# Two keys prepared at the start of the recurrence and split by VectorE, and buffers kept from the recurrence into attention

## What is computed

```python
x = _layernorm(x + _L0_attn_ref(x, ...))              # a selective-scan recurrence (Mamba)
x = _layernorm(x + _L0_xattn_ref(x, ctx, ctx, ...))   # cross attention, 16 heads of 16
x = _layernorm(x + _L0_ffn_ref(x, ...))               # 15 experts, top 3, and a shared expert

# the recurrence: E = 512 channels, N = 16 states, 256 steps
h = exp(d_l[:, :, None] * A) * h + (d_l * x_l)[:, :, None] * B_l[:, None, :]
y_l = einsum('ben,bn->be', h, C_l)

# cross attention
q, k = apply_rope(q), apply_rope(k)                   # x * cos + rotate_half(x) * sin
Q, K, V = q @ Wq.T + bq, k @ Wk.T + bk, v @ Wv.T + bv
out = softmax(Q K^T / sqrt(16)) V;  return out @ Wo.T + bo
```

## Time and profile before

| | |
|---|---|
| median of three executions | 1957.96 us |
| the profiled execution: its time / its span | 1956.72 / 1954.8 us |
| TensorE, VectorE, ScalarE, GpSimd busy | 83%, 76%, 55%, 65% of the span |
| recurrence, from the first scan | 61 to about 943 us |
| attention block | 958 to about 1440 us with the first part of the shared expert |
| feed forward | to the end |
| mean granted TensorE clock | 0.93 of 2.4 GHz |
| DMA | 239 MB, 122 GB/s over the span |

### The profile page before, as it was taken

The page is one execution under the profiler, slowest core; times in us unless marked ns, Lnnn a source line. Parts: engine busy times, 40 slices in busy tenths (PEclk is TensorE's granted clock), DMA queues, the critical chain, the costliest instruction groups (busy, mean ns, idle before and its releaser), DMA issues. The chain is left out here.

```text
span 1954.8 us, 32722 instructions
## 1 busy us (share of the span) xinstructions
PE 1627.6 (83%) x9596; PEld 1045.3 (53%) x9597; DVE 1481.9 (76%) x2438; ACT 1083.9 (55%) x2436; POOL 1266.4 (65%) x942
## 2 busy tenths in 40 slices
PE   7777777788878777874389989998997999999997
PEld 5444444444544444442156666665675556555686
DVE  4999999999999999989668878886532444444478
ACT  4777777777777877775235544444321333333325
POOL 3888888899888889898446888883410333333300
PEclk9789999989899998896689999998998999999999
DMA  7455555444454554444446764442145222222262
GB/s 236 115 117 119 120 130 130 107 110 94 103 126 113 130 130 115 103 97 93 88 125 168 196 185 138 137 136 69 67 177 187 87 84 86 85 85 87 72 263 87
DMA packets 180374, 239.35 MB, mean 122 GB/s; under 512 B 24778, under 2 KB 116813, under 8 KB 178158
## 3 DMA queue, kind: packets, MB, share of 16 engines
q1 hardware_dynamic: 160110, 201.04, 39.5%
q0 software_dynamic: 9888, 27.80, 4.0%
q10 hardware_dynamic: 10240, 8.84, 1.8%
HBM read 173.19 MB, written 65.90 MB: 122 GB/s over the span
## 5 line engine op out<-in xcount | busy, mean ns | idle before, releaser
L348 POOL TENSOR_TENSOR inject<-dx_n,bc_n 128x2048 f32<-128x2048 f32 x127 | 576.0, 4548 | 94.0 <-issue 67.3
L533 ACT ACTIVATE ps_h<-delta_n,a_neg 128x256 f32<-128x256 f32 x1024 | 425.0, 463 | 114.4 <-DVE hc L703 78.6
L690 DVE TENSOR_TENSOR_SCAN ps_h<-ps_h,inject 128x1024 f32<-128x1024 f32 x160 | 365.7, 2286 | 21.0 <-ACT ps_h L533 21.0
L1510 ACT ACTIVATE expT<-ps_t 128x512 f32<-128x512 f32 x256 | 148.5, 596 | 190.2 <-PE ps_t L1995 185.9
L357 POOL TENSOR_TENSOR h_pool<-h_pool,bc_n 128x1024 f32<-128x1024 f32 x96 | 227.2, 2368 | 0.0
L1636 DVE TENSOR_REDUCE neg_max<-ps_s 128x2 f32<-128x512 f32 x256 | 172.4, 680 | 71.4 <-PE ps_s L1984 65.1
L690 DVE TENSOR_TENSOR_SCAN h_pool<-ps_h,inject 128x1024 f32<-128x1024 f32 x96 | 218.5, 2276 | 3.4 <-ACT ps_h L533 3.4
L2641 PE MATMUL ps_uh<-arena,s_xT 128*128 x440 | 210.3, 601 | 5.0 <-issue 4.9
L703 DVE TENSOR_TENSOR hc<-ps_h,bc_n 128x1024 f32<-128x1024 f32 x160 | 195.7, 1223 | 5.9
L2481 DVE TENSOR_TENSOR s_gate<-ps_uh,arena 128x512 f32<-128x512 f32 x110 | 76.1, 692 | 138.6 <-PE ps_uh L2641 138.6
L2370 ACT ACTIVATE s_act<-ps_aa 128x256 f32<-128x256 f32 x110 | 42.3, 384 | 189.8 <-PE ps_aa L2648 189.8
(11 more groups left out here) (332 smaller groups left out, 3387.9 us busy)
## 6 DMA issues: line engine op xcount, KB each, us to landing
delta_n<-dup_rows SPq DMA_DIRECT2D x124, 256.0 KB, 4.6
dx_n<-dup_rows SPq DMA_DIRECT2D x124, 256.0 KB, 7.4
bc_n<-bc_rows SPq DMA_DIRECT2D x64, 256.0 KB, 4.5
xg<-slot_rows SPq DMA_DIRECT2D x110, 136.0 KB, 2.1
Qs<-q_rows SPq DMA_DIRECT2D x192, 64.0 KB, 2.7
arena<-token_results SPq DMA_DIRECT2D x8, 1536.0 KB, 18.5
Ks<-k_rows SPq DMA_DIRECT2D x180, 64.0 KB, 2.7
dup_rows<-delta SPq DMA_DIRECT2D x32, 256.0 KB, 3.7
```

What stands on the lines that cost most here:

```text
L348: nc.gpsimd.tensor_tensor(inject[:, at:at + 2, :, :], dx_n[c // 2][:, None, :, c % 2, :].to_broadcast([P, 2, JB, L]), bc_n[b % 2][:, 0, nq ...
L533: last = nc.scalar.activation(ps_h[k % 2][:, j, :], delta_n[c // 2][:, j, c % 2, :], ACT.Exp, scale=a_neg[:, c, nq, j:j + 1])
L690: nc.vector.tensor_tensor_scan(out.rearrange("p j t -> p (j t)"), ps_h[k % 2][:, :, :].rearrange("p j t -> p (j t)"), inject[:, k % RING, ...
L1510: nc.scalar.activation(expT[:, h % (2 * HG), :, :], ps_t[h % 2][:, :, :], ACT.Exp).then_inc(h_exp, 1)
```

## The change

- `AHEAD` is 2: at the recurrence's beginning two keys are made instead of three. GpSimd only rotates them; VectorE splits both. VectorE's list is now make_dx(0,0), refine(REST), the two splits, make_dx(0,1), first scan. ScalarE computes the root for refine(REST) ahead of `take_k`. One context load fewer is issued.
- At the recurrence's end VectorE splits query 1 too, ahead of the last layer norm's steps; GpSimd ends with the rotations.
- A tensor `common` lives from the recurrence into attention (and its room is reused in feed forward). In the recurrence it holds u[0], skip[0], delta_n[0] and dx_n[0]; in attention cos, sin, Wq, Wk, Qs[0] and Ks[0]. So SP loads cos, sin, Wq and Wk once, during the last sequence, and issues the 12 stack DMAs of key 0 and the first 6 of query 0 (after saving it, and before saving query 1) before the recurrence's block ends. SP waits for each query's save.
- In attention the four `turn_loads` and ScalarE's stacks are gone; ACT's queue issues context 2, context 0, Wv, bv and context 3. GpSimd clears the V buffers, then rotates key 2, splits it (query 2 was its work before), and rotates key 3.
- Key 2 is made in round -1: `project_k(2)` at h 5, `project_q(2)` at h 7 (was 5), `turn_max(0, 0)` at 13 (was 11). Work of round -1's end moves into round 0: `project_v(0)` to h 1, `turn_max(0, 1)` to h 2, `turn_x(3)` to h 3, `project_k(3)` from h 3 to 6 and `project_q(3)` from 5 to 8. VectorE splits query 2 at h 1 of round 0, takes V at 3, rotates query 3 at 5, and splits the output bias at 9, 11, 13, 15 (was 2, 4, 6, 8). SP issues the loads of Wo and bo ahead of two context loads and saves key 2.
- Feed forward: the same instructions on buffers that lie elsewhere.

```diff
@@ recurrence: SP
+            sp.wait_ge(s_inject, inject_count((B - 1) * ITERS + ITERS // 2 - 1))
+            for c in range(DC):
+                stack(qk.Ks, c, qk.k_dram, K_ORDER)
+            sp.wait_ge(s_decay, (B - 1) * ITERS + ITERS // 2)
+            save_q(0)
+            stack(qk.Qs, 0, qk.q_dram, Q_ORDER)
+            save_q(1)
@@ recurrence: GpSimd, begin and end
-            g.wait_ge(qk.got, 16 * 8)
+            g.wait_ge(qk.got, 16 * K_LOADS)
             for n in range(AHEAD):
...
-            split_k(0)
             for p in range(LEAD):
                 make_injects(p)
             g.wait_ge(qk.k_split, AHEAD)
...
-            g.wait_ge(qk.q_made, MADE)
-            g.wait_ge(s_hc, hc_count(B * ITERS - 1))
-            split(q_rows[1], q_parts[1], qk.q_split)
@@ recurrence: ScalarE
             take_delta(0, 0)
+            root(REST, 2)
             take_k(0)
             take_k(1)
             softplus_exp(0, 1)
             softplus_log(0, 1)
             take_delta(0, 1)
-            take_k(2)
-            root(REST, 2)
@@ recurrence: VectorE
             make_dx(0, 0)
+            refine(REST, 2)
+            for n in range(AHEAD):
+                v.wait_ge(qk.kb_made, n + 1)
+                split(k_rows[n], k_parts[n], 18 + 4 * n, qk.k_split)
             make_dx(0, 1)
-            refine(REST, 2)
-            for n in range(1, AHEAD):
-                v.wait_ge(qk.kb_made, n + 1)
-                split(k_rows[n], k_parts[n], 18 + 4 * (n - 1), qk.k_split)
@@ recurrence: TensorE
             project_k(0)
             project_k(1)
             add_softplus(0, 1)
-            project_k(2)
             transposes(1)
@@ attention: SP, GpSimd, ACT
-            stack_q(0, 0)
             stack_q(0, 1)
-            load_ctx(AHEAD)
-            load_ctx(0)
...
-            g.wait_ge(turn_got, TURN)
-            k_rope(AHEAD)
+            for q in range(2):
+                link(nc.gpsimd.memset(V[q][:, :, :, :], 0.0))
+                nc.gpsimd.memset(V[q][:, :, :, DK:DK + 1], 1.0).then_inc(pads_set, 1)
+            k_rope(2)
             split_max(0, 0)
-            split_q(2)
+            split_k(2)
             split_max(0, 1)
+            k_rope(3)
...
-            act.wait_ge(k_saved, 16)
-            stack_k(0)
-            for dst, src in turn_loads:
-                act.dma_start(dst, src).then_inc(turn_got, 16)
-            stack_k(1)
+            act.dma_start(ctxT[2][:, :, :], ctx_v[2]).then_inc(ctx_in[2], 16)
+            act.dma_start(ctxT[0][:, :, :], ctx_v[0]).then_inc(ctx_in[0], 16)
+            for dst, src in late_loads:
+                act.dma_start(dst, src).then_inc(late_got, 16)
+            act.dma_start(ctxT[3][:, :, :], ctx_v[3]).then_inc(ctx_in[3], 16)
+            take_k(2)
             take_q(2)
             take_max(0, 0)
-            take_max(0, 1)
@@ attention: VectorE
-            v.wait_ge(turn_got, TURN)
             rope_q(2)
             add_rope(2)
...
+                    if b == 0 and h == 1:
+                        split_q(2)
+                    if b == 0 and h == 3:
+                        v.wait_ge(late_got, LATE)
+                        take_v(0)
@@ attention: TensorE
                     if b == -1 and h == 5:
-                        pe.wait_ge(turn_got, TURN)
+                        project_k(2)
+                    if b == -1 and h == 7:
                         project_q(2)
+                    if b == 0 and h == 1:
+                        pe.wait_ge(late_got, LATE)
+                        pe.wait_ge(kb_made, 3)
+                        project_v(0)
+                    if b == 0 and h == 3:
+                        pe.wait_ge(v_made, 1)
+                        turn_x(3)
+                    if b == 0 and h == 6:
+                        project_k(3)
+                    if b == 0 and h == 8:
+                        pe.wait_ge(n_made, 2)
+                        project_q(3)
```

More of the change, by code:

```diff
@@ L115, in mamba_phase @@
         zcor = skip_raw
-        u = [sb(f"u{j}", [P, EC, L]) for j in range(2)]
-        skip = [sb(f"skip{j}", [P, EC, L]) for j in range(2)]
+        u = [qk.common[0][:, 0, :, :], sb("u1", [P, EC, L])]
+        skip = [qk.common[0][:, 1, :, :], sb("skip1", [P, EC, L])]
         db = sb("db", [ZK, L])
@@ L123, in mamba_phase @@
         dx = sb("dx", [P, 2, L])
-        delta_n = [sb(f"delta_n{j}", [P, JB, 2, L]) for j in range(2)]
-        dx_n = [sb(f"dx_n{j}", [P, JB, 2, L]) for j in range(2)]
+        delta_n = [qk.common[1][:, :, :, :].rearrange("p a c t -> p (a c) t").rearrange("p (j c) t -> p j c t", c=2),
+                   sb("delta_n1", [P, JB, 2, L])]
+        dx_n = [qk.common[2][:, :, :, :].rearrange("p a c t -> p (a c) t").rearrange("p (j c) t -> p j c t", c=2),
+                sb("dx_n1", [P, JB, 2, L])]
         bc_n = [sb(f"bc_n{j}", [P, 2, NQ, L]) for j in range(2)]
@@ L182, in mamba_phase @@
         EXP_A = 3
+        K_LOADS = 7
         def roots_at(n):
@@ L310, in _, with stack, save_q @@
                                      ).then_inc(qk.k_saved, 16)
+            def stack(to, c, of, order):
+                of_v = of[0].rearrange("(h d) (c a t) -> d c h a t", d=DK, c=DC, a=PARTS)
+                for i, part in enumerate(order):
+                    sp.dma_start(to[i * DK:(i + 1) * DK, c * HC:(c + 1) * HC, :], of_v[:, c, :, part, :]
+                                 ).then_inc(qk.stacked[c], 16)
+            def save_q(n):
+                sp.wait_ge(qk.q_split, n + 1)
+                sp.dma_start(qk.q_dram[n], q_parts[n].rearrange("p c a t -> p (c a t)")).then_inc(qk.q_saved, 16)
+                sp.wait_ge(qk.q_saved, 16 * (n + 1))
             sp.wait_ge(out_done, B - 1)
@@ L807, in _ @@
             v.wait_ge(s_hc, hc_count(B * ITERS - 1))
-            split(q_rows[0], q_parts[0], 18 + 4 * (AHEAD - 1), qk.q_split)
+            for n in range(MADE):
+                if n:
+                    v.wait_ge(qk.q_made, n + 1)
+                split(q_rows[n], q_parts[n], 18 + 4 * (AHEAD + n), qk.q_split)
             for step in rows:
@@ L1173, in __init__ @@
         self.bq, self.bk = sb("bq", [P, DC]), sb("bk", [P, DC])
+        self.whole = sb("common", [P, 3, 2, EC, L])
+        self.common = [self.whole[:, j, :, :, :] for j in range(3)]
+        self.Qs, self.Ks = (self.whole[0:SR + PARTS, j, :, :, :].bitcast(BF16).rearrange("p a c t -> p (a c t)").rearrange(
+            "p (h t) -> p h t", h=NH) for j in (1, 2))
+        self.stacked = [sem(f"stacked{c}") for c in range(DC)]
         self.got, self.chain = sem("got"), sem("chain")
@@ L1197, in sem @@
             return ctx.enter_context(nc.semaphore(name))
-        wq, wk, wv, wo = (sb(n, [P, DC, D]) for n in ("wq", "wk", "wv", "wo"))
+        cos, sin, wq, wk = (front.common[0][:, j // 2, j % 2 * DC:(j % 2 + 1) * DC, :] for j in range(4))
+        wv, wo = sb("wv", [P, DC, D]), sb("wo", [P, DC, D])
         bq, bk = front.bq, front.bk
         bv = sb("bv", [P, D])
-        cos, sin = sb("cos", [P, DC, L]), sb("sin", [P, DC, L])
         ident_bf = sb("ident_bf", [P, P], BF16)
@@ L1621, in set_pads @@
             def set_pads():
-                for q in range(2):
-                    nc.vector.memset(V[q][:, :, :, :], 0.0).then_inc(pads_set, 1)
                 nc.vector.tensor_copy(ident_bf[:, :], ident[:, :]).then_inc(pads_set, 1)
@@ L2105, in _ @@
                         turn_max(b + 1, 0)
-                    if b == -1 and h == 15:
-                        pe.wait_ge(n_made, 1)
-                        turn_max(0, 1)
                     if real(b - 2) and h == 13:
```

147 lines of the change are left out of this document (66 added, 81 removed).

## The result

The changed kernel took 1939.39 us, median of ten executions (1936.31 to 1948.69), against 1956.94 us for the kernel before on the same chip (ten executions, 1952.03 to 1965.91). The ratio is 0.9918, with a 95% interval from 0.9897 to 0.9939: 16 us less, between 12 and 20. The forecast was 11.6 us less, and its range of 1938 to 1952.5 holds the measured time, 1.4 us from its lower end.

What follows compares the result with a forecast made beforehand. The prediction took VectorE to set the recurrence's steady pace and TensorE attention's, both untouched by the change. It summed 1956.72 - 5.7 + 0.5 - 6.4 = 1945.1 us, range 1938 to 1952.5.

Steps and rivals of the forecast that it cites:

- third pair: Recurrence's beginning: GpSimd's third pair of input terms starts at 55.4 instead of 61.17 us, its 5.75 us wait gone.
- Term 1: Recurrence's beginning: VectorE's 10.3 us lead is cut to about 6 by iteration 7; -5.7 us, from -5 to -10.3.
- the lead is kept whole: Rival: recurrence keeps VectorE's 10.3 us, or attention its whole 9 to 11 us; 1940.5 or 1938 us, chance 0.14.
- Recurrence's end: VectorE's split of query 1 and SP's serial list of saves and stacks cost +0.5 us, from 0 to +1.5.
- the first part: Attention's start up to the first exponential: the 12.25 us wait goes, first exponential 9.0 us earlier (-9.0).
- The second part: Attention's round 0, first exponential to take_max of the next sequence: moved-in work less the bo wait, +2.6 us.
- the bo wait: Attention's round 0: VectorE's 3.94 us wait for bo goes, since Wo and bo are issued earlier.
- attention gives nothing: Rival: in round 0 split_q(2) and GpSimd's rotation of key 3 delay each other, 3.9 us; 1951.5 us, chance 0.15.
- the 12.25 us wait: Attention's start: VectorE waits 12.25 us for Wk to land before rotating query 2; claimed to go.
- Nothing is gained anywhere: Rival: the beginning's lead is lost at a sequence boundary where GpSimd waits for dx; 1957 us, chance 0.09.
- Slower: Rival: moved buffers cost GpSimd time in the recurrence, instructions 13% longer, 4 us of loss; 1961 us, chance 0.06.

Runs made afterwards that it cites:

- e1: Changed kernel with project_db(1) put ahead of the sums in iteration 4 of the first sequence; ratio to the kernel before 0.9884 (0.9842 to 0.9926).
- e9: Changed kernel with project_db(1) ahead of the sums, bo's split in round -1 and turn_max(0, 0) at head 11; median 1931.59 us, ratio 0.9877 to the kernel before.
- e3: Changed kernel with cos, sin, Wq and Wk loaded again at attention's start; one execution, 1958.6 us (whole time not used); block to first exponential 28.4 us.
- e5: Changed kernel with bo and Wo loaded at attention's start and bo split at head 5 of round -1; ratio to the kernel before 0.9911 (0.9887 to 0.9934).
- e6: Changed kernel with only bo's split moved, to heads 0, 2, 4 and 5 of round 1; ratio to the kernel before 0.9933 (0.9915 to 0.9952).
- e4: Changed kernel with key 0's stacks issued at attention's start again; one execution, 1957.98 us (whole time not used); block to first exponential 31.2 us.
- e11: The changed kernel itself, unchanged, run again in a later group; median 1938.20 us, ratio to the kernel before 0.9908 (0.9890 to 0.9927).
- e10: Changed kernel with e9's three edits, sequence 3's rotation and projection one head earlier, and maxima (1, 1) split before key 4's rotation; 1931.79 us, ratio 0.9876 to kernel before.
- e2: Changed kernel with refine(REST) put back behind the splits and make_dx(0,1); one execution, 1953.16 us (whole time not used); lead at scan 16 5.2 us.

## Why the prediction was right, and where its working was off

**Recurrence's beginning: right in mechanism, and in size partly by luck.** Forecast: first scan 48.6, third pair 55.4, ScalarE's db near 74, a lead cut from 10.3 to about 6 by iteration 7. Measured: 49.45, 56.1 (51.60 plus one pair of 4.53), 74.61, and 10.3 cut to 7.0 at iteration 7 and 6.3 at 10. The first two are 0.7 to 0.9 late because dx landed at 46.97 instead of 46.29. Term 1 was -5.7 and is -6.3. Two errors cancel in it: the chain that was to carry 5.7 us carried 5.0, and 1.2 us that ScalarE had waited for VectorE behind `db` in the kernel before went too, which the working didn't count. The choice between the two numbers was the largest choice in the sum; e1 shows it was decided by the chain that was named, as that lead stays at 9.4 once `project_db` no longer stands behind GpSimd's product. The rival "the lead is kept whole" named this chain as what speaks against it, and that held.

From scan 50 on the lead wanders: 4.0 at scan 56, then 3.2, 5.6, 5.1, and 7.4 at the last scan. The windows of single sequences show why, in the kernel after and then before (us; busy time of PE, PEld, DVE, ACT and POOL; granted clock, DMA share, GB/s):

```profile
163.60:218.80 55.20, 44.16 (x276) 26.32 (x273) 52.39 (x48) 43.20 (x96) 48.41 (x14) 0.91 0.51 115
218.80:276.30 57.50, 45.46 (x276) 26.46 (x276) 52.55 (x48) 43.56 (x96) 50.90 (x15) 0.91 0.51 113
276.30:332.60 56.30, 46.79 (x279) 27.63 (x280) 52.50 (x48) 43.00 (x96) 50.28 (x16) 0.88 0.49 113
```

```profile
501.70:559.20 57.50, 45.47 (x276) 27.05 (x276) 52.53 (x48) 43.59 (x96) 51.18 (x16) 0.91 0.50 112
...
835.50:893.10 57.60, 38.22 (x248) 21.05 (x248) 52.52 (x48) 40.39 (x89) 50.91 (x15) 0.88 0.49 113
```

From the second on a sequence lasts 55.2 us, but a few in each execution last 1 to 3.5 us more: the ninth and fifteenth in the kernel before (57.5, 57.6), the fourth and fifth in both executions of the changed kernel (57.5 and 56.3, 57.5 and 56.1), the tenth and eleventh in e9 (57.0 and 56.2), the fourth in e3 (58.7). In e1 none lasts more than 55.8. VectorE is not busier in them; it waits for ScalarE's decays (1.25 and 2.21 us, ahead of the scans at 225.9 and 237.6 in the kernel after). Why just these sequences is open: a granted clock of 0.91 stands beside 55.2 as beside 57.5. It makes any lead uncertain by 2 to 3 us.

**Recurrence's end: right.** Forecast +0.5; 17.3 became 17.4. The residual starts at 945.32, 0.2 us behind TensorE's last product, as the split of query 1 ends there, and SP saves query 1 at 947.92 right behind its six stacks.

**Attention: the sum is right to 1 us, its two parts are not.** From the block's start to round 1's first exponential 61.8 us became 54.4, 7.4 less; forecast was 6.4. But the first part, -9.0, is -13.7. The first row maximum came where it was put (3.2 us behind the block's start). Behind it 23.1 us were counted and 18.2 measured. `project_q(2)` took 1.89 us, at a granted clock of 1.00, where 3.6 had been taken from the low clock. GpSimd's key was awaited for 1.01 instead of 2 and the maxima for 1.89 instead of 3. The rest of the 4.9 us, some 1.1, is not parted further.

The second part, +2.6, is +6.3. Up to `take_max(1, 0)` round 0 grew by 1.0 us, and behind it, where the forecast had stopped its count, by 5.3 (from 4.0 to 9.3). That step failed: with bo's split moved from heads 2 to 8 to heads 9 to 15, three of its four pieces went from one side of that mark to the other, and the working costed this move at nothing but the gain of the bo wait. By e5 and e6 the 5.3 us are these three pieces.

Up to the mark the working counted 1.9 + 1.5 + 1.3 + 1.9 us of added work against 3.94 gained, and 1.0 more was measured. Its single terms were not right. `project_v(0)` took 3.38 us, not 1.89. `split_q(2)` took 3.9 us (973.45 to 977.3), not 2.7, one of its subtractions 1.63 us long beside GpSimd's rotation. Both are dearer than was put, and the sum is still smaller. The other side of the same miscount is here: in the kernel before all nine instructions of bo's split, 4.9 us in sum, stood ahead of the mark, in the changed kernel only two, 1.5 us, and the working counted none of that as gained. How the rest is shared out, no run parts.

So "attention gives nothing" was half right: the two engines did hold each other up, though `split_q(2)` lost 1.2 us by it where the rival put 3.9, and round 0 did lose 6.3 us, the amount that rival needed. But it lost 5.3 of them by bo's split, which the rival didn't name, and the start gave 13.7 us instead of 9.0. That the sum of both parts came within 1 us of the forecast is luck: it is 4.7 us too little in one and 3.7 too little in the other, with opposite signs.

**Kept tables and stacks.** The prediction told the 12.25 us wait as one for Wk. e3 and e4 show two waits lying on each other, one for the tables and one for the stacks; either alone costs the first exponential 7 to 10 us.

**The other rivals.** The measured median, 1939.39 us, lies in the band that the prediction gave to "the lead is kept whole" (1937 to 1941, chance 0.14), and not in that of its forecast (1941 to 1950). That rival's mechanism did not happen: the lead was cut, and attention gave 7.4 us in sum. The profiled execution took 1937.66 us where the sum had 1945.1; of these 7.4 us, 2.1 lie ahead of the block's start, 1.0 in attention up to round 1, and 4.3 behind that, which no term foresaw. "Nothing is gained anywhere" needed the lead lost at a sequence's boundary; the wander takes 2 to 3 us and gives them back, in both kernels. "Slower" needed GpSimd's instructions 11% longer; a pair lasts 4.55 us after and 4.55 before, from `common` or from the old place of dx alike (page of the kernel after):

```profile
L364 POOL TENSOR_TENSOR inject<-common,bc_n 128x2048 f32<-128x2048 f32 x63 | 285.6, 4545 | 86.1 <-issue 66.6
L364 POOL TENSOR_TENSOR inject<-dx_n,bc_n 128x2048 f32<-128x2048 f32 x64 | 290.2, 4546 | 0.0
```

**What is left open.** From round 2 to the end, which the change doesn't touch, the profiles last 912.2 us before, 907.0 after, 906.5 in e11, 908.8 in e9 and 911.9 in e10. So up to 5 of the 19 us between the two profiled executions can be this scatter; the 16 us by the ratio of ten executions each are the better number. 14.7 us are seen in the places named, up to round 1's first exponential.

## What to carry to other kernels

When an engine gets a head start, follow the first few steps through every in-order list before counting it: the lead is worth what the tightest chain between the engines lets through, and that chain may be only a matter of order (`project_db` two lines earlier was worth 3 us). A count must run on to a point where all moved work is done; one that stops at a convenient mark misses what was moved past it. Small work costs nearly its own length where its engine is busy throughout (bo's split, 5.3 us in round 0), and nothing that these runs can tell where the engine is seen waiting (e5, round -1): put it there, and load its operands early enough for that. Before calling one order better than another, compare the granted clock of the two stretches: round 0 lasted 32.4 us in e2 and 34.5 in e11, with the same instructions in it.
